# The FFN's first weight factors, moments and z tiles made within the attention's last heads

## The chip, the cores and the metric

One core of a Trainium2 chip runs the whole program. The time is the device time of one execution in microseconds; lower is better. In this text a microsecond is us.

## The reference, cut to what matters

A transformer block with both branches fed by the same layer norm, four batches of 512 tokens.

```python
# L0_attn_x (4, 512, 512); hidden 512, 16 heads of 32, inter 2048
x = L0_attn_x
xn = _layernorm(x)
x = x + attention(xn, Wq, bq, Wk, bk, Wv, bv, Wo, bo) + ffn(xn, gate_cp, up_cp, down_cp)

# attention
q, k, v = proj(Wq, bq), proj(Wk, bk), proj(Wv, bv)
scores = q @ k.T / sqrt(32) + slope[h] * arange(1 - s, 1)   # causal: masked above the diagonal
ctx = softmax(scores) @ v
attn = ctx @ Wo + bo

# ffn: each dense weight is a Catmull-Rom spline through 8134 control points
def spline_reconstruct(control_points, out_size, in_size):
    n = out_size * in_size
    idx, f = _catmull_rom_grid(control_points.shape[0], n)
    p0, p1, p2, p3 = control_points[idx[0]], ..., control_points[idx[3]]
    w = 0.5 * (2*p1 + (p2 - p0)*f + (2*p0 - 5*p1 + 4*p2 - p3)*f**2 + (3*p1 - p0 - 3*p2 + p3)*f**3)
    return w.reshape(out_size, in_size)
inter = silu(xn @ gate_w.T) * (xn @ up_w.T)      # gate_w, up_w (2048, 512)
ffn = inter @ down_w.T                           # down_w (512, 2048)
```

## The kernel before, in words

The program has two blocks, `attention` and `ffn`, each with one hand-written instruction stream per engine (TensorE PE, VectorE DVE, ScalarE ACT, GpSimd POOL, SyncE SP, which issues the DMAs). All engines meet at a barrier between the two. Inside a block only semaphores order the engines; every engine runs its own stream strictly in order.

Every fp32 product is made of two rounded parts, high and low, and three matmuls (high x high, high x low, low x high). So each operand costs a copy on ACT (high) and a subtraction on DVE or POOL (low).

**Attention.** It goes over batches b = 0..3 and heads s = 0..15. One `step(b, s)` does the scores of head s (L513), the exponentials on ACT (L901), transposes the probabilities of head s-2 (`turn_probs`, L527) and multiplies those of head s-3 with the values (`weigh_values`, L544 and L547). Projections of later heads and batches are laid into the steps by the tables `UNITS` and `TURNS`. For the last batch the tables run dry: from step 8 on only the last q and k columns, the turns of the context and the output projection are left. Three extra steps (16 to 18) drain the last heads; `project_out` and `add_residual` (L751) end the block. Three PSUM banks (`pj_bank`) go round for all projections; `PJ_LAST` lists the order in which the last batch uses them. `stack` on SP copies q and k of four heads to their stacked form by three DMAs each (L1048); the fourth stack of a batch serves heads 12 to 15. `load_early` then brings the FFN's mask, the first three `factor`/`taps` chunks and the moment basis `bm_early` into room that the q, k and v weights no longer need.

**FFN.** The weights are never dense in the gate and up products. Four moments per piece of the normalised input ("mom": 21 matmuls with `bm`, L1279 to L1281, their high and low parts, a store to DRAM) and windows of it are loaded as the tile `z` (L1535 windows, L1557 moments); small factors `wgu_hi`, `wgu_lo` multiply it (`gate_up`, "gu", L1303 and L1304, 4 matmuls). The factors come in chunks: seven DVE or POOL operations blend a chunk of `taps` with its `factor` (`taps_op`, L1232 four products and L1237 three sums), ACT rounds (`taps_high`, L1352), DVE or POOL takes the low part (`taps_low`, L1250), and SP copies the halves across partitions (`copy_across`, L1519 or L1524). Chunk 0 gives `coef`, from which the dense down weight is made tile by tile ("gen": `make_down`, 4 matmuls with `bd`, L1291 and L1292; ACT L1358, DVE `merge` L1418, ACT L1367, DVE L1422). Chunks 1 to 4 give the gate and up factors of four tiles each. `down` (12 matmuls, L1316 to L1318) adds a tile to the output.

There are 64 FFN steps k, 16 tiles g for each of four batches t; batch t = 0 is attention batch 3. `ffn_order()` writes PE's order: for t = 0 each step is gu(k), down(k-2), gen(k+2), and the moments of the next batch stand behind two of the steps. Two pairs of PSUM banks alternate; `room_for` makes PE wait until the pair's last user is read. Before, POOL blends chunks 1 and 4, DVE chunks 0, 2 and 3. SP's FFN stream is one list of waits and DMAs; a wait in it holds all that follows.

## Time and profile before

| | us |
|---|---|
| median of 3 runs | 844.9 (841.9 to 845.68) |
| profiled execution, whole time | 845.87 |
| its span, first to last instruction | 844.1 |
| PE busy in the span | 703.6 (83%) |
| DVE, ACT, POOL busy | 505.1, 439.5, 354.6 |

The span is what the engines' records cover; the whole time is 1.8 us longer. The profiled execution lies 1.0 us above the median of the three runs. In the page's row of 40 slices of 21.1 us each, PE's digit is 8 or 9 nearly everywhere, 4 and 1 in two slices in the middle, at the change from attention to FFN. Matmuls overlap in the records (one lasts 0.39 us, the next starts after 0.23 us), so a stretch's rate is read from its count.

### The profile page before, as it was taken

The page shows a single profiled execution, that of the slowest core. Times are in us where ns is not written, and L with a number is a line of the kernel's source. Part 1 is how long each engine was busy: PE and PEld are TensorE (multiplying, and loading weights), DVE is VectorE, ACT ScalarE, POOL GpSimd, SP SyncE. Part 2 cuts the span into 40 slices and gives each one's busy share as a digit, 9 for nine tenths or more (in the row PEclk, how much of TensorE's full clock was granted, in tenths as well). Part 3 has the DMA queues.
Part 4 walks back from the last instruction along what each step waited for, and adds up shares of the span by engine and source line. Part 5 has one row for each costly group of instructions (what it writes and reads, how often), then busy time and mean ns, then how long its engine had stood idle before and what let it go on. Part 6 is the DMA issues. An engine that isn't in the chain of part 4 may idle for free. (4 is left out here: it accounts for less than half of the span.)

```text
span 844.1 us, 14059 instructions
## 1 busy us (share of the span) xinstructions
PE 703.6 (83%) x4884; PEld 558.1 (66%) x4884; DVE 505.1 (60%) x1273; ACT 439.5 (52%) x961; POOL 354.6 (42%) x207
## 2 busy tenths in 40 slices
PE   5677879889789898798898684169895999999997
PEld 4566657667567676576776563147684888888886
DVE  5286687779968888877798767185341321221212
ACT  4267566677748776666778751135441233233221
POOL 2343363445535444634455435145223334434434
PEclk9879689999989999899899798569997999999999
DMA  7982564454585336644545917664617545434401
GB/s 252 207 205 37 101 92 153 58 88 75 114 202 76 50 69 134 92 153 58 89 73 124 319 74 246 230 212 136 184 23 228 174 148 175 140 92 138 133 1 50
DMA packets 53024, 109.79 MB, mean 130 GB/s; under 512 B 6361, under 2 KB 6617, under 8 KB 51417
## 3 DMA queue, kind: packets, MB, share of 16 engines
q1 hardware_dynamic: 52808, 108.82, 51.6%
q8 instruction: 39, 0.64, 0.4%
q14 instruction: 33, 0.26, 0.1%
q10 hardware_dynamic: 144, 0.07, 0.0%
HBM read 59.32 MB, written 25.17 MB: 100 GB/s over the span
## 5 line engine op out<-in xcount | busy, mean ns | idle before, releaser
L988 POOL TENSOR_TENSOR work<-work 128x1280 f16<-128x1280 f32 x64 | 168.4, 2630 | 228.3 <-DVE work L714 228.1
L901 ACT ACTIVATE work<-work,neg_max 128x128 f32<-128x128 f32 (+3 forms) x256 | 142.2, 564 | 105.5 <-DVE neg_max L706 104.7
L706 DVE CUSTOM_DVE_ANT_0 work<-bank,dist 128x128 f32<-128x128 f32 (+3 forms) x256 | 115.4, 487 | 82.5 <-PE bank L513 68.2
L1476 POOL TENSOR_TENSOR in_lo<-inner,in_hi 128x512 fp32r<-128x512 f32 x64 | 84.0, 1313 | 180.5 <-ACT in_hi L1379 180.5
L1430 DVE TENSOR_TENSOR inner<-bank,silu 128x512 f32<-128x512 f32 x64 | 44.1, 689 | 135.7 <-ACT silu L1373 122.4
L910 ACT COPY work<-bank 128x768 f16<-128x768 f16 (+1 forms) x128 | 110.3, 909 | 28.5 <-PE bank L527 27.2
L527 PE MATMUL bank<-ident,work 128*128 128x128 f16 x1280 | 109.9, 231 | 10.3 <-DVE work L721 8.5
L513 PE MATMUL bank<-k_stack,q_stack 96*128 96x256 f32 (+2 forms) x256 | 81.6, 397 | 41.5 <-issue 22.5
L1379 ACT CAST in_hi<-inner 128x512 fp32r<-128x512 f32 x64 | 39.8, 621 | 146.4 <-PE bank L1318 137.6
L527 PEld LDWEIGHTS bank<-ident,work 128*128 128x128 f16 x1280 | 78.6, 103 | 50.4 <-issue 33.2
L1316 PE MATMUL bank<-w_room,in_hi 128*128 128x512 f32 x256 | 100.9, 394 | 0.4 <-POOL in_lo L1476 0.4
L1317 PE MATMUL bank<-w_room,in_hi 128*128 128x512 f32 x256 | 100.4, 392 | 0.0
L1318 PE MATMUL bank<-w_room,in_lo 128*128 128x512 f32 x256 | 100.3, 392 | 0.0
L513 PEld LDWEIGHTS bank<-k_stack,q_stack 96*128 96x128 f32 x256 | 48.9, 212 | 59.4 <-issue 31.2
L544 PE MATMUL bank<-v_parts,work 128*128 128x96 bf16 x640 | 68.1, 215 | 5.1 <-issue 3.9
L1303 PE MATMUL bank<-z,wgu_hi 128*128 128x512 f32 x128 | 52.2, 408 | 19.1 <-DMA z<-moment_scratch 9.3
L472 PE MATMUL bank<-xt_room,w_room 128*128 128x512 f32 x128 | 61.9, 484 | 5.1 <-DVE v_room L682 3.2
L547 PE MATMUL bank<-v_parts,work 128*128 128x64 bf16 x640 | 65.4, 199 | 0.0
L544 PEld LDWEIGHTS bank<-v_parts,work 128*128 128x128 f16 x640 | 53.8, 103 | 9.3 <-issue 4.7
L1316 PEld LDWEIGHTS bank<-w_room,in_hi 128*128 128x128 f32 x256 | 48.7, 190 | 11.5 <-POOL in_lo L1476 1.3
L1317 PEld LDWEIGHTS bank<-w_room,in_hi 128*128 128x128 f32 x256 | 48.7, 190 | 10.3
L1318 PEld LDWEIGHTS bank<-w_room,in_lo 128*128 128x128 f32 x256 | 48.5, 189 | 10.3
(101 smaller groups left out, 1429.0 us busy)
## 6 DMA issues: line engine op xcount, KB each, us to landing
q_stack<-parts SPq DMA_DIRECT2D x48, 256.0 KB, 5.6
k_stack<-parts SPq DMA_DIRECT2D x48, 256.0 KB, 5.6
z<-xt_scratch SPq DMA_DIRECT2D x128, 88.0 KB
x_in<-x SPq DMA_DIRECT2D x32, 256.0 KB, 5.7
xt_scratch<-xt_room SPq DMA_DIRECT2D x8, 1024.0 KB, 6.8
xt_room<-xt_scratch SPq DMA_DIRECT2D x6, 1024.0 KB, 8.2
factor<-c_basis SPq DMA_DIRECT2D x5, 1024.0 KB, 9.7
taps<-windows SPq DMA_DIRECT2D x5, 1024.0 KB, 11.6
```

The costliest lines, as they stand in the source:

```text
L513: pe.matmul(score_bank[i % 2][:, 0:n], q_stack[:, c % 2, h, i * P:(i + 1) * P], k_stack[:, c % 2, h, 0:n], start=True, stop=True).then_inc ...
L527: mm = pe.transpose(pt_bank[i % 2][:, (part * n + k) * P:(part * n + k + 1) * P], probs16[:, s % 2, part, OFF[i] + k * P:OFF[i] + (k + 1) ...
L544: pe.matmul(bank[:, i * 96:(i + 1) * 96], probs_t[:, s % 2, at:at + P], v_parts[:, k, s, :, :], start=(k == 0), stop=False)
L547: mm = pe.matmul(bank[:, i * 96:i * 96 + 64], probs_t[:, s % 2, at:at + P], v_parts[:, k, s, 0:2, :], start=False, stop=(k == n - 1))
L706: dve.tensor_tensor_reduce(probs[:, s % 2, OFF[i]:OFF[i] + n], score_bank[i % 2][:, 0:n], dist[:, S - n:S], -slope(s), 3.4e38, ALU.add, AL ...
L901: e = act.activation(tile, tile, ACT.Exp, bias=neg_max[:, s % 2, i:i + 1], scale=-1.0, accum_out=row_sum[:, s % 4, i:i + 1])
L910: act.copy(probs_t[:, s % 2, 2 * OFF[i]:2 * OFF[i] + n], pt_bank[i % 2][:, 0:n]).then_inc(pt_free[i % 2], 1)
L988: pool.tensor_tensor(probs16[:, s % 2, 1, :], probs[:, s % 2, :], probs16[:, s % 2, 0, :], ALU.subtract).then_inc(lo_ready, 1)
L1316: pe.matmul(sum_bank[i][:, :], hi, wd_hi[:, g, :], start=(g == 0), stop=False)
L1317: pe.matmul(sum_bank[i][:, :], hi, wd_lo[:, g, :], start=False, stop=False)
L1318: mm = pe.matmul(sum_bank[i][:, :], lo, wd_hi[:, g, :], start=False, stop=(g == NG - 1))
L1476: pool.tensor_tensor(in_lo[:, k % 2, :], inner[:, k % 2, :], in_hi[:, k % 2, :].bitcast(F32), ALU.subtract).then_inc(il_ready, 1)
```

## The change

SBUF rooms of the FFN are placed by hand at offsets from the end of the common rooms, over attention tensors by when these are last read: `wgu_hi` over `q_stack`, `wgu_lo` over `k_stack`, `bd` and `z` over the probabilities and values, `coef` over `dist` and `bv_all`, and `in_lo` in two pieces.

- `load_basis` (the moment basis and `factor` 2) is issued ahead of the last `stack`; the mask goes behind chunks 0 and 1.
- PE makes the last batch's three moments at the ends of steps 12, 13 and 14 (9, 9 and 3 matmuls); ACT takes the high part in the same step, DVE the low part at the end of the next. SP stores them, and then loads the first `bd` quarter, the windows of z tiles 0 to 3 once all probabilities are transposed, their moments, and the second `bd` quarter, all within the attention block.
- DVE blends chunks 0 and 1 in steps 17 and 18 and between the last four residual sums; ACT rounds them and issues their copies on its own DMA queue, behind the loading of the Silu table.
- In the FFN, chunks 2, 3 and 4 all go through DVE by the table `TAPS`, spread over steps k = 0 to 10; POOL blends nothing. The next batch's moments move from behind steps 8 and 9 to behind 11 and 13.
- SP's list for t = 0 is rewritten: loads of z tiles, chunks and copies alternate; `bm`, the next batch's `xt_room`, the residual and the last `bd` quarter now stand together ahead of the last copy.

The diff, cut to its core ("..." where lines are left out; the helpers `taps_op`, `tiles_of`, `taps_low`, `load_windows` and `load_moments` moved out of `ffn` with their bodies as they were):

```diff
+        base = aligned(nc)
+        room = lambda name, shape, dt, at: nc.alloc_sbuf_tensor_at(name, shape, dt, offset=base + at * KB)
+        wgu_hi = room("wgu_hi", [P, 2, NG, P], F32R, 0)
+        wgu_lo = room("wgu_lo", [P, 2, NG, P], F32R, 16)
+        bd = room("bd", [P, 2, 4, 2, P], F32R, 32)
+        z = room("z", [P, NG, S], F32R, 42)
+        coef = room("coef", [P, 2, 512], F32R, 74)
+        in_lo = [room("in_lo0", [P, S], F32R, 78), room("in_lo1", [P, S], F32R, 40)]
...
+        def load_basis(sp):
+            sp.wait_ge(bases_st, 16)
+            sp.dma_start(bm_early[:].bitcast(F32).rearrange("p k e n -> p (k e n)"), moment_d).then_inc(bme_ld, 16)
+            sp.dma_start(factor[2][:], c_factor[2]).then_inc(chunk_ld[2], 16)
+
         def load_early(sp):
 
-            sp.dma_start(mask.bitcast(U32).rearrange("p g n -> p (g n)"), c_mask).then_inc(mask_ld, 16)
             for c in range(2):
                 sp.dma_start(factor[c][:], c_factor[c]).then_inc(chunk_ld[c], 16)
                 sp.dma_start(taps[c][:], cpts[c]).then_inc(chunk_ld[c], 16)
-            sp.wait_ge(bases_st, 16)
-            sp.dma_start(bm_early[:].bitcast(F32).rearrange("p k e n -> p (k e n)"), moment_d).then_inc(bme_ld, 16)
-            sp.dma_start(factor[2][:], c_factor[2]).then_inc(chunk_ld[2], 16)
+            sp.dma_start(mask.bitcast(U32).rearrange("p g n -> p (g n)"), c_mask).then_inc(mask_ld, 16)
...
+        def copy_across(eng, c):
+
+            eng.wait_ge(made_lo[c], 2)
+            for m in range(2):
+                own, other = slice(m * ZR, (m + 1) * ZR), slice((1 - m) * ZR, (2 - m) * ZR)
+                if c == 0:
+                    eng.dma_start(coef[other, m, :].bitcast(F32), in_lo[0][own, :].bitcast(F32)).then_inc(dup_ld[0], 16)
+                    continue
+                for each in (wgu_hi, wgu_lo):
+                    tiles = each[:, m, 4 * (c - 1):4 * c, :].rearrange("p g n -> p (g n)")
+                    eng.dma_start(tiles[other].bitcast(F32), tiles[own].bitcast(F32)).then_inc(dup_ld[c], 16)
...
+MOMENTS = {12: 0, 13: 1, 14: 2}
+PJ_LAST = [("q", 3), ("k", 3), ("c", 1), ("m", 0), ("m", 1), ("m", 2), ("c", 2), ("o", 0), ("o", 1), ("c", 3), ("o", 2), ("o", 3)]
...
+            def moment(m):
+                bank, used = pj_use(("m", m), B - 1)
+                pe.wait_ge(pj_free[bank], used)
+                if m == 0:
+                    pe.wait_ge(bme_ld, 16)
+                some = [(n, c) for n, (of, c) in enumerate(BM_PAIRS) if of == m]
+                for n, c in some:
+                    first, last = n == some[0][0], n == some[-1][0]
+                    pe.matmul(pj_bank[bank][:, :], bm_early[:, n, 0, :], xt_hi[:, c, :], start=first, stop=False)
+                    pe.matmul(pj_bank[bank][:, :], bm_early[:, n, 0, :], xt_lo[:, c, :], start=False, stop=False)
+                    mm = pe.matmul(pj_bank[bank][:, :], bm_early[:, n, 1, :], xt_hi[:, c, :], start=False, stop=last)
+                mm.then_inc(pj_full, 1)
...
+                if s in MOMENTS:
+                    moment(MOMENTS[s])
...
+                if s - 1 in MOMENTS:
+                    moment_low(MOMENTS[s - 1])
+                if s == H + 1:
+                    for n in range(4):
+                        taps_op(dve, 0, n)
+            for n in range(4, 7):
+                taps_op(dve, 0, n)
             ctx_low(B - 1, KC - 1)
-            for q in range(QT):
-                add_residual(B - 1, q)
+            taps_op(dve, 1, 0)
+            add_residual(B - 1, 0)
+            dve.wait_ge(ql_ready, 8 * B)
+            for m in range(2):
+                taps_low(dve, 0, m)
+            add_residual(B - 1, 1)
+            for n in range(1, 4):
+                taps_op(dve, 1, n)
+            add_residual(B - 1, 2)
+            for n in range(4, 7):
+                taps_op(dve, 1, n)
+            add_residual(B - 1, 3)
+            for m in range(2):
+                taps_low(dve, 1, m)
...
+            def moment_high(m):
+                bank, _ = pj_use(("m", m), B - 1)
+                act.wait_ge(pj_full, pj_total(("m", m), B - 1))
+                if m < 2:
+                    act.wait_ge(stacked[m][(KC - 1) % 2], 2 * STACK * B)
+                else:
+                    act.wait_ge(mom_sv[0], 32)
+                act.copy(parts[:, 2 * (m % 2), :], pj_bank[bank][:, :]).then_inc(mom_hi, 1)
...
+            act.wait_ge(t_done, 4 * H * B)
+            taps_high(act, 0)
             act.activation(warm[:], ident[0:1, 0:1], ACT.Silu)
+            copy_across(act, 0)
+            act.wait_ge(s_full, 4 * H * B)
+            taps_high(act, 1)
+            copy_across(act, 1)
...
+            load_basis(sp)
             stack(B - 1, 3)
...
+            for m in range(3):
+                bank, used = pj_use(("m", m), B - 1)
+                sp.wait_ge(pj_free[bank], used + 1)
+                per = 8 if m < 2 else 4
+                for e in range(2):
+                    sp.dma_start(mom_d[2 * (B - 1) + e, :, 8 * m:8 * m + per, :],
+                                 parts[0:NG * per, 2 * (m % 2) + e, :].bitcast(F32)).then_inc(mom_sv[m % 2], 16)
+            sp.wait_ge(lo_ready, H * B)
+            load_pieces(sp, 0)
+            sp.wait_ge(pt_full, QT * H * B)
+            sp.wait_ge(xt_st, 32 * B)
+            sp.wait_ge(pad_st, 16)
+            for g in range(4):
+                load_windows(sp, 0, g)
+            sp.wait_ge(mom_sv[0], 64)
+            sp.wait_ge(mom_sv[1], 32)
+            load_moments(sp, 0, 0)
+            load_pieces(sp, 1)
             for q in range(QT):
...
-    order = [("mom", 0, 0, 0), ("mom", 0, 1, 1), ("gen", 0, 0, 1), ("gen", 1, 0, 1)]
+    order = [("gen", 0, 0, 1), ("gen", 1, 0, 1)]
...
-        if t < B - 1 and g in ((8, 9) if t == 0 else (6, 8)):
-            half = 0 if g == (8 if t == 0 else 6) else 1
+        if t < B - 1 and g in ((11, 13) if t == 0 else (6, 8)):
+            half = 0 if g == (11 if t == 0 else 6) else 1
...
+TAPS = {0: [(2, i) for i in range(4)], 1: [(2, i) for i in range(4, 7)], 2: [(2, 7), (3, 0)], 3: [(3, 1), (3, 2)],
+        4: [(3, 3), (3, 4)], 5: [(3, 5), (3, 6)], 6: [(3, 7), (4, 0)], 7: [(4, 1), (4, 2)], 8: [(4, 3), (4, 4), (4, 5)],
+        9: [(4, 6)], 10: [(4, 7)]}
+HIGHS = {1: 2, 5: 3, 9: 4}
...
             sp.dma_start(taps[2][:], cpts[2]).then_inc(chunk_ld[2], 16)
-            sp.wait_ge(xt_st, 32 * B)
-            sp.wait_ge(pad_st, 16)
-            for q in range(QT):
-                sp.wait_ge(res_st[q], 16 * B)
-            load_pieces(0)
-            for g in range(4):
-                load_windows(0, g)
-            load_chunk(4)
-            load_pieces(1)
-            load_chunk(3)
-            copy_across(0)
-            for m in range(3):
-                store_moment(0, m)
-            load_moments(0, 0)
-            copy_across(1)
-            sp.dma_start(bm[:].bitcast(F32).rearrange("p k e n -> p (k e n)"), moment_d).then_inc(bm_ld, 16)
-            copy_across(2)
-            load_xt(1)
             for g in range(4, 8):
                 load_windows(0, g)
             load_moments(0, 1)
+            for q in range(QT):
+                sp.wait_ge(res_st[q], 16 * B)
+            load_chunk(3)
+            copy_across(sp, 2)
+            sp.dma_start(taps[4][:], cpts[4]).then_inc(chunk_ld[4], 16)
+            for g in range(8, 12):
+                load_windows(0, g)
+            load_moments(0, 2)
             load_pieces(2)
             sp.wait_ge(made[3], 4)
-            sp.nop(nofuse=True)
+            sp.dma_start(factor[4][:], c_factor[4]).then_inc(chunk_ld[4], 16)
+            copy_across(sp, 3)
+            for g in range(12, NG):
+                load_windows(0, g)
+            load_moments(0, 3)
+            sp.dma_start(bm[:].bitcast(F32).rearrange("p k e n -> p (k e n)"), moment_d).then_inc(bm_ld, 16)
+            load_xt(1)
+            sp.wait_ge(made[4], 4)
             load_mid(0)
-            copy_across(3)
-            sp.wait_ge(made_lo[4], 2)
-            sp.nop(nofuse=True)
-            for g in range(8, 16):
-                load_windows(0, g)
-                if g % 4 == 0:
-                    load_moments(0, g // 4)
-            copy_across(4)
             load_pieces(3)
+            copy_across(sp, 4)
```

DVE at the end of the attention, before: the low part of the last context column, then the four residual sums.

```order
L744 TENSOR_TENSOR ctx_t<-bank,ctx_t 128x512 [waits ch_ready]
L751 TENSOR_TENSOR x_in<-bank,x_in 128x512 [waits res_ld0,pj_full]
L751 TENSOR_TENSOR x_in<-bank,x_in 128x512 [waits res_ld1,pj_full]
L751 TENSOR_TENSOR x_in<-bank,x_in 128x512 [waits res_ld2,pj_full]
L751 TENSOR_TENSOR x_in<-bank,x_in 128x512 [waits res_ld3,pj_full]
```

DVE at the same place after the change (`taps_52` is chunk 0, `taps_53` chunk 1; four products of chunk 0 stand one head earlier):

```order
L335 TENSOR_TENSOR taps_52<-taps_52 128x512 [waits made0] x3
L846 TENSOR_TENSOR ctx_t<-bank,ctx_t 128x512 [waits ch_ready]
L330 TENSOR_TENSOR taps_53<-taps_53,factor_50 128x512 [waits chunk_ld1]
L853 TENSOR_TENSOR x_in<-bank,x_in 128x512 [waits res_ld0,pj_full]
L355 TENSOR_TENSOR in_lo_61<-taps_52,coef 64x512 [waits made_hi0,ql_ready]
L355 TENSOR_TENSOR in_lo_61<-taps_52,coef 64x512 [waits made_hi0]
L853 TENSOR_TENSOR x_in<-bank,x_in 128x512 [waits res_ld1,pj_full]
L330 TENSOR_TENSOR taps_53<-taps_53,factor_50 128x512 x3
L853 TENSOR_TENSOR x_in<-bank,x_in 128x512 [waits res_ld2,pj_full]
L335 TENSOR_TENSOR taps_53<-taps_53 128x512 [waits made1] x3
L853 TENSOR_TENSOR x_in<-bank,x_in 128x512 [waits res_ld3,pj_full]
L355 TENSOR_TENSOR wgu_lo<-taps_53,wgu_hi 64x512 [waits made_hi1] x2
```

Between and behind the residual sums now stand the blends of both chunks and their low parts; the last two rows before the barrier are chunk 1's low parts, each 64 rows high.

SP in the FFN's first batch, before: what stands around the last `bd` quarter, which PE's gen 12 to 15 need.

```order
L1535 DMA z<-xt_scratch 44x1x512 x8
L1557 DMA z<-moment_scratch 20x4x512 x2
L1535 DMA z<-xt_scratch 44x1x512 x6
L1524 DMA wgu_hi<-wgu_hi 64x512 [waits made_lo4]
L1524 DMA wgu_lo<-wgu_lo 64x512
L1524 DMA wgu_hi<-wgu_hi 64x512
L1524 DMA wgu_lo<-wgu_lo 64x512
L1509 DMA bd<-bases_scratch 128x1024 [waits gen_full]
```

SP after the change, around the same load:

```order
L367 DMA wgu_hi<-wgu_hi 64x512
L367 DMA wgu_lo<-wgu_lo 64x512
L317 DMA z<-xt_scratch 44x1x512 x8
L322 DMA z<-moment_scratch 20x4x512 x2
L1669 DMA bm<-bases_scratch 128x1792
L1634 DMA xt_room<-xt_scratch 128x4x512 x2
L1642 DMA resid<-mid_scratch 128x512 [waits made4]
L1642 DMA resid<-mid_scratch 128x512 x3
L309 DMA bd<-bases_scratch 128x1024 [waits gen_full]
L367 DMA wgu_hi<-wgu_hi 64x512 [waits made_lo4]
```

The last `bd` quarter stood behind z windows and a copy; it now stands behind z windows, the basis `bm`, two loads of `xt_room` and four of `resid`. The copy of chunk 4 stands behind it.

## Rows read from the trace of the kernel before

**Rows 1.** Windows view: us, busy time and count of each engine, PE clock, DMA.
```profile
517.70:539.80 22.10, 0.01 (x1) 0.01 (x1) 10.05 (x10) 1.82 (x3) 6.20 (x4) 0.57 0.89 319
539.80:564.10 24.30, 11.41 (x24) 6.66 (x24) 14.83 (x21) 7.60 (x13) 7.04 (x5) 0.57 0.50 144
564.10:637.80 73.70, 70.21 (x293) 56.11 (x293) 36.34 (x51) 35.26 (x61) 26.34 (x19) 0.97 0.48 141
637.80:647.10 9.30, 0.06 (x1) 0.01 (x1) 0.00 (x0) 0.62 (x1) 6.13 (x5) 0.64 0.84 251
647.10:652.10 5.00, 4.98 (x15) 3.97 (x16) 0.69 (x1) 0.60 (x1) 0.00 (x0) 0.64 0.61 170
700.00:750.00 50.00, 49.78 (x220) 40.91 (x219) 12.01 (x18) 15.41 (x28) 20.54 (x17) 1.00 0.45 134
```

**Rows 2.** Timeline, PE: start, duration, instruction, idle before and its releaser.
```profile
472.84 0.77 PE L513 MATMUL bank<-k_stack,q_stack 96*128 96x256 f32 x2 [4.20 <-issue]
539.79 0.80 PE L1291 MATMUL bank<-coef,bd 128*128 128x512 f32 x1 [22.11 <-DVE mom_st L1409]
564.14 0.80 PE L1303 MATMUL bank<-z,wgu_hi 128*128 128x512 f32 x1 [0.80 <-DVE inner L1430]
600.89 0.50 PE L1279 MATMUL bank<-xt_room,bm 128*128 128x512 f32 x1 [1.51 <-DVE w_new L1418]
647.12 0.77 PE L1303 MATMUL bank<-z,wgu_hi 128*128 128x512 f32 x1 [9.27 <-DMA z<-moment_scratch]
```

**Rows 3.** Timeline, ACT and DVE, the FFN's start.
```profile
538.42 0.59 ACT L1345 CAST mom_st<-bank 128x512 fp32r<-128x512 f32 x1 [12.61 <-DMA moment_scratch<-mom_st]
541.90 0.59 ACT L1358 COPY w_new<-bank 128x512 f32<-128x512 f32 x1 [2.89 <-PE bank L1292]
542.59 0.72 DVE L1418 COPY_PREDICATED w_new<-v_room,bank 128x512 f32<-128x512 uint8 x1 [2.85 <-ACT w_new L1358]
```

**Rows 4.** Timeline, PE and DVE, between attention heads 14 and 15.
```profile
485.26 0.96 PE L527 MATMUL bank<-ident,work 128*128 128x128 f16 x14 [0.68 <-DVE work L721]
486.03 0.48 PE L513 MATMUL bank<-k_stack,q_stack 96*128 96x256 f32 x2
486.80 0.29 DVE L706 CUSTOM_DVE_ANT_0 work<-bank,dist 128x128 f32<-128x128 f32 x1
```

**Rows 5.** Timeline, DVE, the attention's last operation.
```profile
511.10 0.69 DVE L751 TENSOR_TENSOR x_in<-bank,x_in 128x512 f32<-128x512 f32 x1 [2.10 <-PE bank L474]
```

**Rows 6.** View of the tile taps: durations min/median/max in ns, first and last start.
```profile
L1232 DVE TENSOR_TENSOR taps<-taps,factor x12: 676/687/1825, 512.6 to 564.0; 128x512 f32<-128x512 f32 x12
L1232 POOL TENSOR_TENSOR taps<-taps,factor x8: 1280/1714/1737, 512.6 to 568.1; 128x512 f32<-128x512 f32 x8
```

**Rows 7.** Timeline, SP: start and duration of DMA issues.
```profile
448.48 3.63 SPq L1053 DMA_DIRECT2D x_in<-x  x4
458.65 1.87 SPq L1048 DMA_DIRECT2D q_stack<-parts  x3
464.28 2.97 SPq L1048 DMA_DIRECT2D k_stack<-parts  x3
547.06 0.60 SPq L1524 DMA_DIRECT2D wgu_lo<-wgu_lo  x1
630.50 0.36 SPq L1626 DMA_DIRECT2D bo_all<-bo  x1
631.98 6.76 SPq L1535 DMA_DIRECT2D z<-xt_scratch  x8
638.84 0.81 SPq L1557 DMA_DIRECT2D z<-moment_scratch  x2
```

**Rows 8.** DMA view, issues at 467.4, 470.3, 604.5 us: KB, us to landing.
```profile
v_room<-c_mask SPq DMA_DIRECT2D x1, 1024.0 KB, 7.7
...
factor<-c_basis SPq DMA_DIRECT2D x1, 1024.0 KB, 20.3
...
bd<-bases_scratch SPq DMA_DIRECT2D x1, 512.0 KB, 3.9
```

292 lines of the change are left out of this document (133 added, 159 removed).

## The prediction

> **What bounds the kernel now.** I read four views. First the page's row of 40 slices, to see where PE is idle: two slices at the change from attention to FFN. Then the windows view over these places [rows 1]: from 517.7 to 539.8 us PE does one matmul, from 539.8 to 564.1 it does 24, from 564.1 to 637.8 it does 293, then it stands 9.3 us. At full rate, 220 matmuls in 50 us give 0.227 us each. The last batches run at that rate, so work moved inside them gains nothing and only the idle stretches can be won. Third the timeline, for what ends each idle. PE's 22.1 us before 539.79 are put down to DVE's `mom_st` [rows 2]; ACT's row shows the true end: the third moment's high part waited 12.61 us for the store of the first, since `mom_st` has two slots [rows 3], and SP issued that store behind its list of loads. Beside it POOL and DVE blend together from 512.6 on, and an operation of DVE lasts up to 1.8 us instead of 0.69 [rows 6]. Fourth SP's timeline and the DMA view: the boundary to the second FFN batch waits for z's moments, issued at 638.84 as the end of a chain that begins when gen 15 ends, at 630.5 [rows 2, 7].
>
> **The change, part by part.** The sum is made against the profiled execution: 845.87 us, span 844.1.
>
> Attention, loads. `bm_early` and `factor` 2, 1.9 MB, now go out behind the residual loads, at about 452 us, ahead of the last q and k stacks (458.65 and 464.28). For the k stack PE waited 4.2 us, until 472.84 [rows 2, 7]. Seven loads that landed 7.7 us after 467.4 (the first) and 20.3 us after 470.3 (the last) moved 5.9 MB in 15.5 us, 2.65 us a MB [rows 8]; so 1.9 MB take 5.0 us and could be through when q's stack is issued at 458.7. Bounds 0 and 5 us; I take 1.0, as most of it falls in a gap.
>
> Attention, moments. A head's last transposes end at 486.03 where the next scores start; DVE takes these at 486.80, some 0.5 us after they are there, because it is itself busy [rows 4]. Nine matmuls are 2.05 us, so DVE starts 1.55 us late, less 0.25 in step 12, where it has a context column to finish. The 0.69 us low part fits into the wait of the following head. The last moment has three matmuls (0.7 us) that fit under DVE, but the low parts of the second and third then stand bare: 0.65 us each. Sum 1.3 + 1.6 + 1.3 = 4.2. ACT's three copies of 0.6 us lie in the same waits. Bounds: 1.9 (only the DVE operations) and 8 (whole matmul time plus all copies and low parts). PE's tail moves 5.2 us.
>
> Attention, tail. The last residual sum stood at 511.10 to 511.8, behind an idle of 2.1 us, as DVE has little to do there [rows 5]; the FFN began at 512.6 [rows 6]. DVE's blend of chunk 0 (products 2.5, sums 2.0) fits before and behind the normalising of head 15. Then DVE has, between the residual sums, 0.6 + 1.4 + 1.9 + 2.0 us, which keep up with PE until the third residual sum; the fourth ends at 518.0 instead of 517.0. Behind it: ACT's two casts, 0.6 each and starting at the same time as that sum (1.3); DVE's low parts 1.4; then ACT issues four copies at 0.6, 2.4; barrier 0.4 [rows 3, 6, 7]. FFN start at about 522.8, so +10.2 against 512.6. Bounds 517 (nothing of it bare) and 528. SP has 6.8 us of windows, moments and `bd` in hand from about 502 and is through before the last residual store.
>
> FFN start. gen 0 is PE's first instruction, at 522.9 instead of 539.79: gain 16.9. From gen 0 to gu(2) before: 564.14 - 539.79 = 24.35. Now, in order, at the low clock (four matmuls 2.1 us, 539.79 to ACT's start at 541.90): gen 0 2.1, ACT 0.6, merge 0.72, gen 1 beside which ACT rounds (to 5.6), gu(0), directly behind and so 0.4 shorter, to 7.3; ACT's second copy and merge to 7.1; rounding, silu, product to 9.2; DVE four products 2.5 and merge to 12.4; ACT's rounding and silu to 13.6; product to 14.5, gu(2). Every unit is from [rows 3, 6]; what is gone are the waits for POOL's low parts of chunk 1 and for their copy. Gain 9.85. At gu(2) the lead is 26.7.
>
> First FFN batch. 293 matmuls took 73.7 us before; at 0.227 they are 66.5, the rest is the low clock, two waits of 1.51 before the moments [rows 2] and small ones. The moments move but stay two waits. DVE per step: 0.69 + 0.74 + 0.69 and at most three blends, 4.2 of 4.54 us, so it holds. The copy of chunk 2 lands about 1.0 late for gu(4). What POOL loses there nobody waited for.
>
> The last `bd` quarter. From gu(6), in us: product 2.3, low parts 1.4, four copies 2.4, windows 6.8, moments 0.8, `bm` at 13.7, `xt_room`, `resid`, then `bd` at 17.4. In front of it in the queue are 0.9 + 2 + 1 MB; with its own half 4.4 MB x 2.65 = 11.6, so it lands at 25.3 to 27.7. PE needs it for gen 12 at 4 x 4.54 + 0.9 + 2.7 = 21.8. Bounds: in an empty queue it lands 3.9 us after issue [rows 8], no wait; at the other end 10. I take 4.7.
>
> What does the clock do in that wait? After 9.3 us idle, PE did 15 matmuls in 5.0 us instead of 22 at a granted clock of 0.64, 1.6 us lost [rows 1]; after 1.51 us at 600.89 it lost nothing. 4.7 lies between, and I add the 1.6 (sum 6.3), because the idle stretch from 517.7 on has the low clock in most of it. The Trainium skill ("TensorE: Matmul & The Clock Gate", What's actually happening) says the clock falls back after the array has been idle for a while and is released by activity. By it a wait of 4.7 us costs the 1.6 too; a shorter wait, under the lower bound of the landing, costs none.
>
> Boundary. Before: gen 15's end, 0.05 to `bo_all`, `xt_room`, windows 6.76, moments, landing: 16.6 us, of which PE had 7.3 of work [rows 2, 7]. Now the second half of the moments stands behind gen 15: a wait of 1.5, 0.7 of matmuls, ACT 0.6, DVE 0.7, two stores 1.2 on SP before that chain starts. That is 4.7 us more for SP against 2.2 for PE in the same place (already counted): gap 9.3 becomes about 11.5, cost 2.2, bounds 0 and 5. Later batches are the same code.
>
> Sum: 26.7 - 1.0 - 6.3 - 2.2 = 17.2. 845.9 - 17.2 = 828.7 for the profiled execution, which stood 1.0 above the median: 827.7.
>
> **Rivals.**
> (a) The `bd` load passes the backlog and lands in time. For it: z windows of one queue come in among larger loads; against it: the seven loads of [rows 8] landed in their order. Gain 6.3 more: 821.
> (b) The stacks wait behind the 1.9 MB by the full 5 us and the blends' tail runs to 528: 4 + 5 lost, 837. For it: PE waits for the k stack already. Against it: the 6 us between their issue and q's stack.
> (c) DVE becomes the bound. It now blends chunk 4 too while POOL makes `in_lo`. If its 27 blends and low parts in steps 0 to 10 took 1.75 us as beside POOL before, not 0.69 [rows 6], a step with two blends needs 2.1 + 3.5 = 5.6 us against 4.54, one with three 7.4: over the eleven steps 9 steps lose 1.1 to 3, some 18 in all, and the ramp 4. The gain turns into a loss: 850. It decides from 1.5 us a blend on. Against it: POOL works 1.3 us in a step of 4.54, after DVE's turn. The Trainium skill ("GPSIMD Engine Reference", Specifications) says that GpSimd shares its SBUF interfaces with VectorE when the latter's operation has two SBUF inputs, as every blend has. By that rule, each collision is real, and the times of 1.7 agree; what it leaves open is how many there are.
> (d) The change doesn't do what it says: something loaded early (chunk 0, a moment's store that ACT waits for in step 14) comes late and attention stalls. Half of the lead at gu(2) goes: 840.
>
> **Chances.** Forecast 0.50 (own range 824 to 832), (a) 0.22, (b) 0.12, (c) 0.04, (d) 0.08, smaller mixtures 0.04. About 0.5%, 4 us, is what a measurement can tell. Faster by more than that is everything but (c), part of (d) and the rest: 0.92; within 0.03, slower 0.05. The range reaches from (a) with a light attention to (b): 817 to 838.
>
> **What would show it.** Right: gen 0 near 523, gu(2) near 537, a PE wait for DMA `bd` at gen 12 around 577, a gap of 11 to 12 us before the second batch, ending near 630. Wrong: gen 0 after 530; DVE blends of 1.7 us between k = 0 and 10; no wait at gen 12; a PE idle of several us in heads 12 to 15.

## The result and the profile after

| | before | after |
|---|---|---|
| median, us (14 runs each) | 844.98 (840.85 to 847.82) | 839.96 (837.12 to 842.63) |
| profiled execution, whole time | 845.87 | 842.63 |
| its span | 844.1 | 840.8 |

The ratio of after to before is 0.9941, 95% interval 0.9924 to 0.9957: 5.0 us faster, where 17.2 were forecast, and outside the range (817 to 838). The profiled execution of after stands 2.7 us above its median, so the account below is made against 842.63 and the forecast's 828.7, which is 13.9 us apart.

The windows view of the changed kernel, over the stretches that answer to [rows 1]: the attention's end, gen 0 to gu(2), gu(2) to the end of the first batch, the gap (PE's idle ahead of the second batch), and 5 us behind it. A row holds the stretch and its length, the busy time and count of PE, its weight loads, DVE, ACT and POOL, PE's mean granted clock (1.00 is 2.4 GHz, 0.50 is 1.2), the busy share of the DMA engines and their GB/s.

```profile
509.84:524.87 15.03, 7.40 (x30) 5.51 (x31) 10.22 (x16) 3.81 (x6) 0.00 (x0) 0.90 0.66 191
524.87:540.06 15.19, 9.45 (x24) 5.73 (x24) 8.88 (x13) 5.15 (x10) 1.59 (x1) 0.72 0.79 261
540.06:630.90 90.84, 75.13 (x293) 58.48 (x293) 47.22 (x66) 36.41 (x63) 21.02 (x14) 0.89 0.47 143
630.90:643.04 12.14, 0.00 (x1) 0.03 (x1) 0.00 (x0) 0.62 (x1) 6.13 (x5) 0.65 0.90 286
643.04:648.04 5.00, 5.00 (x12) 3.94 (x13) 0.69 (x1) 0.60 (x1) 0.00 (x0) 0.50 0.65 189
```

The first two rows carry the gain: 24 matmuls that took 24.3 us now take 15.19, and PE's idle of 22.1 us is 6.8, so that gu(2) comes 24.1 us sooner (540.06 for 564.14). The third gives most of it back: the same 293 matmuls take 90.84 us instead of 73.70. PE's timeline says where; these rows answer to [rows 2].

```profile
474.40 0.77 PE L600 MATMUL bank<-k_stack,q_stack 96*128 96x256 f32 x2 [4.41 <-issue]
524.87 0.76 PE L1414 MATMUL bank<-coef,bd 128*128 128x512 f32 x1 [6.80 <-PEq L474]
540.06 0.79 PE L1426 MATMUL bank<-z,wgu_hi 128*128 128x512 f32 x1 [0.64 <-DVE inner L1542]
596.79 0.76 PE L1414 MATMUL bank<-coef,bd 128*128 128x512 f32 x1 [10.05 <-DMA bd<-bases_scratch]
606.06 0.50 PE L1402 MATMUL bank<-xt_room,bm 128*128 128x512 f32 x1 [1.86 <-DVE w_new L1530]
643.04 0.77 PE L1426 MATMUL bank<-z,wgu_hi 128*128 128x512 f32 x1 [12.14 <-DMA z<-moment_scratch]
```

The first row is the restart behind the k stack, the second gen 0, the third gu(2), the fourth gen 12, the fifth the first moments of the second batch, the last that batch's gu(0). gen 0 (forecast 522.9) and gu(2) (forecast 537.4) are 2.0 and 2.7 us late. From gu(2) to the restart at 643.04 it takes 103.0 us, before it took 83.0 [rows 2], and the forecast was 92.5. So 10.5 of the 13.9 us are lost in the first FFN batch, and the wait of 10.05 for `bd` is the largest piece. SP's timeline shows how that load came so late.

```profile
568.96 0.54 SPq L367 DMA_DIRECT2D wgu_hi<-wgu_hi  x1
...
571.47 6.56 SPq L317 DMA_DIRECT2D z<-xt_scratch  x8
578.08 0.88 SPq L322 DMA_DIRECT2D z<-moment_scratch  x2
579.00 0.35 SPq L1669 DMA_DIRECT2D bm<-bases_scratch  x1
579.40 0.96 SPq L1634 DMA_DIRECT2D xt_room<-xt_scratch  x2
580.41 4.57 SPq L1642 DMA_DIRECT2D resid<-mid_scratch  x4
585.03 0.50 SPq L309 DMA_DIRECT2D bd<-bases_scratch  x1
```

gu(6) stood at 562.50. The copies were issued 6.5 us behind it (3.7 in the forecast's list). From `bm` to `bd` it is 6.0 us, most of it the four `resid` loads (3.7 in the forecast), and `bd` landed 11.8 us behind its issue.

### The profile page after: what moved, and what is told of

Read it like the earlier page. It is cut to its first block and busy times, and to the rows that moved or that the text cites. A ratio compares the mean times of both kernels' runs of the same rounds, so it can differ in the third digit from the quotient of the medians.

```text
span 840.8 us, 14002 instructions
## 1 busy us (share of the span) xinstructions
PE 707.4 (84%) x4884; PEld 561.4 (67%) x4884; DVE 507.8 (60%) x1289; ACT 439.6 (52%) x961; POOL 332.6 (40%) x191
## 5 line engine op out<-in xcount | busy, mean ns | idle before, releaser
L1579 POOL TENSOR_TENSOR in_lo<-inner,in_hi 128x512 fp32r<-128x512 f32 x64 | 85.8, 1342 | 230.1 <-ACT in_hi L1497 230.1
L1439 PEld LDWEIGHTS bank<-w_room,in_hi 128*128 128x128 f32 x256 | 49.2, 192 | 11.8 <-POOL in_lo L1579 1.3
```

The costliest lines, as they stand in the source:

```text
L1439: pe.matmul(sum_bank[i][:, :], hi, wd_hi[:, g, :], start=(g == 0), stop=False)
L1579: pool.tensor_tensor(in_lo[k % 2][:, :], inner[:, k % 2, :], in_hi[:, k % 2, :].bitcast(F32), ALU.subtract).then_inc(il_ready, 1)
```

## The experiments

Every ratio is to the kernel before, on the same chip, with its 95% interval; the changed kernel alone is 0.9941 (0.9924 to 0.9957). A thousandth is 0.84 us. A, B and C are the theories of the expectation printed above each result. Where the interval of an experiment overlaps that of the kernel it starts from, the times alone don't show its gain, and the reading rests on the profile.

**1. `bd` early.** In SP's list of the first batch:

```
 copy_across(sp, 3)
+load_pieces(3)
 ...
 load_mid(0)
-load_pieces(3)
```

> One move on the sync engine's list of the first FFN batch: the load of the last quarter of bd stands right behind the copy of chunk 3, ahead of the windows of z 12 to 15, bm, xt_room and resid, instead of behind them all. Theory A (the wait at gen 12 is the backlog of 3.9 MB in front of bd plus its late issue, and nothing else stands behind it): bd is issued near 570 instead of 585 and is there long before gen 12, PE's wait of 10.05 us goes, and with it the low granted clock of 596.8 to about 605, worth 3 to 4 us more. The windows and bm then land about 1.5 us later, still ahead of their use. Gain 12 to 14 us against the changed kernel: 826 to 828, ratio to the kernel before about 0.979. Theory B (something else is as late as bd: the second moments' xt_room, or z 12 to 15, behind the same backlog): PE waits there in its place, gain under 5 us, 835 or more. Theory C (the time is set by how much the queue moves between 570 and 597, since the moments of the second batch need bm and xt_room anyhow): the boundary gap of 12.1 us grows by what gen 12 gains, 838 to 841.

Measured 0.9825 (0.9797 to 0.9852), 830.0 us: 9.8 us better than the changed kernel. PE's wait for `bd` is gone; gu(2) to the next batch's start is 91.5 us instead of 103.0. From PE's timeline, the two longest waits behind gu(2):

```profile
596.09 0.50 PE L1402 MATMUL bank<-xt_room,bm 128*128 128x512 f32 x1 [1.86 <-DVE w_new L1530]
...
632.28 0.77 PE L1426 MATMUL bank<-z,wgu_hi 128*128 128x512 f32 x1 [11.37 <-DMA z<-moment_scratch]
```

What follows: `bd`'s place cost 10 to 11.5 us, clock included. That is A with less gain than it said: it laid the low clock from 596.8 to about 605 on this wait, but in the changed kernel's profile the clock is back at 1.00 from 601 to 606 and falls a second time at the moments, as it does here. B and C are out: nothing took the wait's place, and the gap did not grow.

**2 and 3. `bd` in two places between.** In the first it stands ahead of the four `resid` loads, in the second ahead of `xt_room` too.

```
 load_xt(1)                    +load_pieces(3)
 sp.wait_ge(made[4], 4)         load_xt(1)
+load_pieces(3)                 sp.wait_ge(made[4], 4)
 load_mid(0)                    load_mid(0)
-load_pieces(3)                -load_pieces(3)
```

> From the changed kernel, bd's last quarter goes one place forward: ahead of the four resid loads (1 MB), still behind bm and xt_room (3 MB). It is issued at about 580.4 instead of 585.0. Theory A (bd lands when what is queued in front of it has moved, at the 0.31 to 0.39 MB a us that the engines move from 580 to 595): 3.4 MB and the rest of z's windows take some 10 to 11 us from 580, so it lands at 590 to 592 instead of 596.8; PE's wait falls from 10.05 to 4 or 5 us, and still brings the low clock: gain 5 to 6, ratio about 0.987. Theory B (a wait of half the length brings none of the low clock): gain 8, 0.984. Theory C (the landing is set by the slow transfers beside it, not by its place): gain under 2, 0.993.

> bd's last quarter one place further forward: behind bm (0.9 MB) and ahead of xt_room and resid. Theory A (place in the queue): issued at 579.4, lands at 584 to 585, ahead of PE's need at 586.7: no wait, the same as when it stood behind the copy of chunk 3, ratio 0.982 to 0.983. Theory B (z 12 to 15 and xt_room then become what PE waits for): a wait of some us at gu 12 or at the second batch's moments, ratio 0.986 or more.

Measured 0.9892 (0.9860 to 0.9923) and 0.9811 (0.9776 to 0.9846). PE's timeline of the one and of the other:

```profile
592.38 0.77 PE L1414 MATMUL bank<-coef,bd 128*128 128x512 f32 x1 [5.85 <-DMA bd<-bases_scratch]
```
```profile
585.94 0.47 PE L1414 MATMUL bank<-coef,bd 128*128 128x512 f32 x1 [0.95 <-DMA bd<-bases_scratch]
```

The wait goes 10.05, 5.85, 0.95, 0 as the load moves forward from the changed kernel's place, and the issue 22.5, 18.0, 16.9, 9.0 us behind gu(6). From the first place to the second it is issued 4.6 us sooner and lands 12.0 instead of 11.8 us later, though 1 MB less stands in front: what counts there is the issue. Ahead of `xt_room` it lands 8.2 us behind its issue. What is measured is the place in the list (A). Between the first two, 4.2 us less wait gave 4.1 us by the ratios. The profiles show the clock's share: from gen 12 to the first moments it takes 9.27 us behind the wait of 10.05, 8.93 behind 5.85 and 7.56 behind 0.95, where the clock stays at 1.00. So the low clock costs 1.7 us after the longest wait and 1.4 after the middle one (B fell).

**4. The windows of the second batch early.**

```
 copy_across(sp, 4)
+for g in range(4):
+    load_windows(1, g)      # no longer behind the moments' stores
```

> One move: the windows of z 0 to 3 of the second FFN batch are loaded right behind the copy of chunk 4, ahead of the stores of the second batch's moments and of bo_all and xt_room, instead of behind them. Theory A (the gap of 12.14 us before the second batch is the chain stores, bo_all, xt_room, eight window loads at 0.85 us, moments, landing on the one issuing engine): the eight issues, 6.7 us, leave the chain, the moments are issued at about 628 instead of 634.6, and the gap falls to about 6, plus less time at the low clock: 833 to 834. Theory B (the landing of the z moments waits for the 2 MB of xt_room in front of it in the queue): 2 MB at 2.65 to 4 us a MB are 5 to 8 us from 626.9, so the moments land at 632 to 635 plus their own whatever their issue; the gap shrinks by some 3 to 6. Theory C (the gap has its cause in the moments themselves): no change, 840.

Measured 0.9906 (0.9872 to 0.9940), 3.0 us, the gap 7.99 instead of 12.14.

```profile
638.12 0.77 PE L1426 MATMUL bank<-z,wgu_hi 128*128 128x512 f32 x1 [7.99 <-issue]
```

That is B: the issues left the chain, and 2.2 MB in front of the moments took their place. The moments are issued at 627.20, and PE starts 10.9 us behind that.

**5. The moments ahead of those 2.2 MB as well.**

```
 store_moment(1, 2)
+load_moments(1, 0)
 bo_all <- bo ; load_xt(2)
 ...
-load_moments(1, 0)
```

> From the changed kernel, only the boundary: z's windows 0 to 3 of the second batch behind the copy of chunk 4, and its first moments loaded right behind their last store, ahead of bo_all and the 2 MB of xt_room for the third batch. Theory A (with the windows moved alone, ratio 0.9906, the gap fell only from 12.1 to 8.0 us, since the moments then waited for bo_all and xt_room in the queue: 2.2 MB, issued at 609.9 and moments landed 10.8 us behind their issue in the kernel with four moves): the moments are issued 1.6 us earlier and land in about 3 us, so that the gap falls to about 1 and the low clock behind it goes: 10 to 13 us below the changed kernel, 828 to 830, ratio about 0.981. Theory B (the gap is then set by the stores' own chain, since the last store is issued at about 625 and must land before the moments are loaded, 3 + 3 us): gap 2 to 4, 831 to 833, ratio 0.985. Theory C (z 4 to 7 or xt_room come late instead): PE waits later in the second batch, 835 or more.

Measured 0.9811 (0.9779 to 0.9844), 11.0 us.

```profile
631.10 0.47 PE L1426 MATMUL bank<-z,wgu_hi 128*128 128x512 f32 x1 [1.43 <-issue]
```

The gap is 1.43 us instead of 12.14, the whole of A; the moments are issued at 626.71, 4.4 us ahead of that start.

**6. The moments one head earlier in attention.**

```
-MOMENTS = {12: 0, 13: 1, 14: 2}
+MOMENTS = {11: 0, 12: 1, 13: 2}
```

> The three early moments stand one head earlier in attention: the first behind step 11, where PE waits 4.4 us for the k stack, the second in step 12, the third in step 13. Theory A (what the moments cost in attention is PE time, and the first cost double since it ran at the low clock that followed that wait): the first one fills the wait, step 12 carries 9 matmuls at nearer full clock, step 13 three. Before the move heads 12, 13 and 14 were 3.8, 1.6 and 0.5 us longer; now 0, 1.6 to 2.5 and 0.5, so the FFN starts 3 to 4 us earlier, near 521: 836 to 837. Theory B (it is the copies and low parts on ACT and DVE that lengthen the heads): they are all still there, gain below 1 us. Theory C (the low clock comes from the wait for the k stack however it is filled): step 12 stays slow, gain about 2.

Measured 0.9918 (0.9891 to 0.9944). PE's wait for the k stack is 1.86 us, as the nine matmuls now stand ahead of it (1.98 and 3.52 in experiments 10 and 11, which have this move too), and the three heads from 12 to 15 take 15.6 us instead of 18.5. But from head 15's first operation on DVE to the last `ctx_t` it takes 18.9 us instead of 17.0, so most of that is given back. By the ratio 1.9 us are gained, but the two intervals overlap: likely, not shown.

**7. A third of the moments' matmuls.**

```
-some = [... for n, (of, c) in enumerate(BM_PAIRS) if of == m]
+some = [... if of == m][:1]
```

> The first and second early moment in attention are made of 3 matmuls each instead of 9, so this kernel leaves out two thirds of their sums; everything else (copies, low parts, stores, loads) stays. Theory A (a head of attention is longer by the matmul time of its moment, at whatever clock it then runs): in the changed kernel the first moment's nine took 2.86 us from 479.44 to 482.30, most of it at the low clock, the second's 2.05. Without six of each, 1.4 to 2.2 and 1.4 us go: gain 3 to 3.5, some 836.5. Theory B (DVE's and ACT's copies of the moments lengthen the heads): gain under 1 us, 839.5.

This kernel leaves out six of the nine matmuls of the first moment and of the second. Measured 0.9924 (0.9897 to 0.9950), again a difference inside the intervals; the profile tells more than the times. DVE's first operation in heads 12, 13 and 14, before:

```profile
473.53 0.29 DVE L706 CUSTOM_DVE_ANT_0 work<-bank,dist 128x128 f32<-128x128 f32 x1 [5.80 <-PE bank L513]
478.30 0.28 DVE L706 CUSTOM_DVE_ANT_0 work<-bank,dist 128x128 f32<-128x128 f32 x1
482.53 0.29 DVE L706 CUSTOM_DVE_ANT_0 work<-bank,dist 128x128 f32<-128x128 f32 x1
```

after, with head 15's:

```profile
475.08 0.29 DVE L808 CUSTOM_DVE_ANT_0 work<-bank,dist 128x128 f32<-128x128 f32 x1 [6.13 <-PE bank L600]
482.72 0.29 DVE L808 CUSTOM_DVE_ANT_0 work<-bank,dist 128x128 f32<-128x128 f32 x1 [2.79 <-issue]
488.78 0.29 DVE L808 CUSTOM_DVE_ANT_0 work<-bank,dist 128x128 f32<-128x128 f32 x1 [1.23 <-issue]
493.55 0.28 DVE L808 CUSTOM_DVE_ANT_0 work<-bank,dist 128x128 f32<-128x128 f32 x1
```

and with three matmuls a moment:

```profile
471.47 0.29 DVE L808 CUSTOM_DVE_ANT_0 work<-bank,dist 128x128 f32<-128x128 f32 x1 [6.29 <-PE bank L600]
476.34 0.29 DVE L808 CUSTOM_DVE_ANT_0 work<-bank,dist 128x128 f32<-128x128 f32 x1
481.10 0.27 DVE L808 CUSTOM_DVE_ANT_0 work<-bank,dist 128x128 f32<-128x128 f32 x1
```

Head 12 takes 4.77 us before, 7.64 after and 4.87 here; head 13 4.23, 6.06 and 4.76. In head 13 the clock is full in both, and six matmuls cost 1.3 us. In head 12 the 2.8 are not the matmuls alone: behind PE's restart the low clock lasts some 6.5 us in the changed kernel's profile and some 3.6 here (windows of 1 us). The kernel of experiment 2 has all nine matmuls, and there it lasts 3.7:

```profile
476.20 0.29 DVE L808 CUSTOM_DVE_ANT_0 work<-bank,dist 128x128 f32<-128x128 f32 x1 [6.32 <-PE bank L600]
482.48 0.29 DVE L808 CUSTOM_DVE_ANT_0 work<-bank,dist 128x128 f32<-128x128 f32 x1 [1.42 <-issue]
```

That head 12 takes 6.28 us, 1.4 more than with three. So the matmul time is what lengthens the heads (A), 1.3 to 1.4 us for six, and up to 1.4 more is the clock; the ten profiles that have all nine there show head 12 between 6.28 and 7.72 us.

**8. Basis loads behind the k stack.**

```
-load_basis(sp)
 stack(B - 1, 3)
+load_basis(sp)
```

> The loads of bm_early and factor 2 (1.9 MB) are issued behind the last k stack instead of in front of the last q and k stacks, still ahead of the other early loads. Theory A (in front, they cost the k stack more than the profile of the changed kernel shows: PE's wait for it was 4.41 us there, but 5.50, 6.27 and 8.25 in three kernels with the same code up to there, as the basis still moves when q's stack is issued): the wait returns to about 4.2 and the mean gain is 1.5 to 2.5 us, 837.5 to 838.5. bm_early lands at about 473 to 476, in time for the first moment at 479. Theory B (the wait for the k stack is lengthened by whatever is queued behind it, chunk 0's loads in the one case and the basis in the other): no change, 840. Theory C: bm_early comes late for the first moment and head 13 waits, 841 or more.

Measured 0.9966 (0.9947 to 0.9985), and PE's wait 4.46 us. No gain, by the middle value 2 us worse: A's gain is not there. The short wait that A named is, but it shows nothing: PE's wait for the k stack lay between 4.41 and 8.25 us (mean 5.7) in ten profiles whose code is the changed kernel's up to there, three of them under 4.5. What makes it vary was not settled.

**9. Chunk 1's copies in the FFN.**

```
 taps_high(act, 1)
-copy_across(act, 1)
 ...                          # first in SP's FFN list:
+copy_across(sp, 1)
```

> The four copies of chunk 1's factors to the other half of the partitions are issued by the sync engine as the first of the FFN, instead of by ACT in front of the barrier. Theory A (ACT's six DMA issues of 0.5 to 0.6 us stand bare between the last low part at 521.4 and the barrier): the FFN starts 2.2 us earlier, gen 0 at about 522.7, while the copies are issued from then on and land before gu(0) needs them, some 8 us behind gen 0: 837.5 to 838. Theory B (gu(0) then waits for the copies, 4 x 0.8 us of issue and 2 to 3 of landing, and chunk 2's taps come 3 us later to DVE): the gain is given back by gu(2), 840.

Measured 0.9905 (0.9876 to 0.9933), 3.0 us. The intervals overlap, but the profile shows the same 3.0:

```profile
518.71 0.76 PE L1413 MATMUL bank<-coef,bd 128*128 128x512 f32 x1 [3.81 <-PEq L474]
```

From the attention's last `ctx_t` (507.40) to gen 0 PE needs 11.3 us instead of 14.3, and gu(2) is 15.2 us behind gen 0 as in the changed kernel: A, nothing is given back.

**10. Four of these together** (1, 4, 6, 9).

> Four moves together, each tried alone before: bd's last quarter behind the copy of chunk 3 (ratio 0.9825 to the kernel before), z's first windows of the second batch ahead of its moments' stores (0.9906), the early moments one head earlier (0.9918), and chunk 1's copies issued by the sync engine in the FFN (0.9905). The changed kernel alone stands at 0.9941. If they are independent their gains add: 9.8 + 3.0 + 2.0 + 3.0 = 17.8, so 822 (0.973). If the earlier bd and the earlier windows meet in the same queue, or the first batch's start waits for chunk 1, a part is lost: 824 to 827.

Measured 0.9738 (0.9709 to 0.9767), 821.4 us, where the four gains one by one add up to 0.973: they add.

**11. All five** (with 5).

> All moves together: the four of the kernel at 0.9738 and the first moments of the second batch ahead of bo_all and xt_room. Theory A (the gap of 7.92 us there was the queue in front of the moments): it falls to 1 or 2, 7 to 9 us less with the clock: 812 to 814, ratio 0.963 to 0.965. Theory B (the wait only moves to z 4 to 7, which now have 2.2 MB in front of them, or to the moments of the third batch): 817 to 820.

Measured 0.9607 (0.9577 to 0.9636), 812.1 us, a little below A. The gap is 1.36 us.

**12 and 13. Gen ahead of down, then the moments ahead of both**, in the two steps that carry the second batch's moments.

```
 gu(k), down(k-2), gen(k+2), mom        # as it is
 gu(k), gen(k+2), down(k-2), mom        # 12, with bd early
 gu(k), mom, down(k-2), gen(k+2)        # 13, on all five
```

> bd's last quarter early as in the run before, and in the two steps with the second batch's moments the matmuls of gen stand ahead of those of down, so that down's 12 matmuls (2.7 us) lie between gen and the moments, which wait for gen's merge. Theory A (the waits of 1.86 and 1.50 us there are bare, and the first of them drops the granted clock, 0.60 in the 4 us behind it with 11 matmuls instead of 18): both waits go, 3.4 us, and 1.6 with the clock: 5 us below bd early alone, 825. Theory B (down then waits for DVE or ACT, which get the gen's work earlier and the product later): gain under 2 us, 828 or more. Theory C (the second batch's start hangs on the store chain on the sync engine and not on PE): 3.4 us go, but the gap before the second batch grows by 1.5 or more: 828.

> On the kernel with five moves (ratio 0.9607): in the two steps with the second batch's moments, these stand directly behind gu, ahead of down and gen, so that they wait for nothing (the pair of banks was merged a step before) and down's 2.7 us lie between them and gen, which needs the banks next. Theory A (the waits of 1.86 and 1.51 us go, and since no wait is left the clock does not fall behind the first: in the kernel with bd early it was 0.60 for 4 us with 11 matmuls instead of 18): 3.4 + 1.6 = 5 us, 807, ratio 0.955. Theory B (gen now waits for DVE's low parts of two moments, 0.6 + 0.7 + 0.7 behind PE's 4.1, less what down covers): the waits move, as they did with gen ahead of down: gain under 1.5, ratio 0.959 or more. Theory C (bm or xt_room is not there yet): a wait for DMA.

In both, A fell. The first is 0.9860 (0.9832 to 0.9888), no better than `bd` early alone, and its waits ahead of the moments are 2.43 and 2.08 us instead of 1.86 and 1.50. The second is 0.9660 (0.9636 to 0.9685), 4.5 us worse than the five. Its timeline has both of the rivals named, C and B:

```profile
586.13 0.77 PE L1401 MATMUL bank<-xt_room,bm 128*128 128x512 f32 x1 [2.85 <-DMA xt_room<-xt_scratch]
...
598.63 0.50 PE L1413 MATMUL bank<-coef,bd 128*128 128x512 f32 x1 [2.57 <-DVE mom_st L1520]
...
613.16 0.50 PE L1413 MATMUL bank<-coef,bd 128*128 128x512 f32 x1 [1.97 <-DVE mom_st L1520]
```

**14. Small blends.** On the changed kernel.

```
+w = slice(0, 8 if c > 2 else 512)
-taps[c][:, n, :] = taps[c][:, n, :] * factor[c][:, n, :]
+taps[c][:, n, w] = taps[c][:, n, w] * factor[c][:, n, w]   # sums alike
```

This kernel leaves out 504 of the 512 columns of every product and sum of chunks 3 and 4.

> From the changed kernel: the products and sums of chunks 3 and 4 are done on 8 of their 512 columns, so this kernel leaves out nearly all of that work on the vector engine; the casts, low parts, copies, waits and loads stay. Theory A (my rival of a bound vector engine, in a small size: between gu(3) and gu(8) a step takes 4.53 to 5.63 us, 25.6 us for the five of them, against 4.54 for one in which PE waits for nothing): the steps fall to 4.54 except where ACT's casts or the low parts stand, and the kernel gains 2 to 3 us, ratio about 0.991. The copy of chunk 3 is still issued at the same step, and PE's wait for bd stays near 10. Theory B (the longer steps come from ACT's two casts, which stand ahead of gen's copy, and from the clock): under 0.8 us, ratio 0.993 to 0.995.

Measured 0.9940 (0.9915 to 0.9965), the changed kernel's own. From gu(3) to gu(8) it is 24.9 us instead of 25.6. A fell, for these two chunks; chunk 2's blends were left whole.

**15. Casts behind gen's copy.** On all five.

```
 inner_high(n)
-if n in HIGHS: taps_high(act, HIGHS[n])
 ...
 down_start(n)
+if n - 2 in HIGHS: taps_high(act, HIGHS[n - 2])
```

> On the kernel with five moves (ratio 0.9607): ACT's two casts of chunks 2, 3 and 4 stand behind its copy of gen, in the 0.87 us in which it waits for the merge, instead of ahead of that copy. Theory A (ahead of it they delay gen's merge and with it the next product: the steps that carry casts take 5.2 to 6.3 us instead of 4.54): 0.6 to 0.9 us less in two or three steps, 2 us in all, ratio about 0.9585. Theory B (the vector engine's blends stand in the same steps and bound them): no change, 0.9607. Theory C (the copies of the chunks go out later and PE waits for them): slower by 1.

Measured 0.9566 (0.9542 to 0.9590), 808.6 us, the lowest; its interval touches that of the kernel with five moves (0.9577 to 0.9636). ACT's timeline of the changed kernel around gen 7 and, under it, of this one around the same chunk's casts:

```profile
562.93 1.26 ACT L345 CAST wgu_hi<-taps 64x512 fp32r<-64x512 f32 x2 [0.46 <-DVE taps L335]
564.22 0.59 ACT L1474 COPY w_new<-bank 128x512 f32<-128x512 f32 x1
565.67 0.62 ACT L1485 CAST w_room<-w_new 128x512 fp32r<-128x512 f32 x1 [0.87 <-DVE w_new L1530]
```
```profile
554.57 0.59 ACT L1473 COPY w_new<-bank 128x512 f32<-128x512 f32 x1 [0.23 <-PE bank L1414]
555.05 1.26 ACT L345 CAST wgu_hi<-taps 64x512 fp32r<-64x512 f32 x2
556.34 0.62 ACT L1484 CAST w_room<-w_new 128x512 fp32r<-128x512 f32 x1
```

The 0.87 us in which ACT waited for the merge now holds most of the casts: from the copy to its rounding it is 1.77 us instead of 1.45, for casts of 1.26. The windows from gu(2) to gu(12), first of the kernel with five moves, then of this one:

```profile
534.70:595.80 61.10, 55.45 (x219) 43.19 (x219) 40.51 (x56) 28.94 (x50) 17.00 (x11) 0.93 0.68 214
```
```profile
533.37:590.51 57.14, 54.35 (x219) 43.35 (x219) 40.21 (x56) 28.75 (x50) 17.21 (x11) 0.93 0.72 225
```

The same instructions take 4.0 us less, and the ratios differ by 3.5. The 4.0 lie in the steps that begin with gu(2), (3), (6), (7) and (10), 0.6 to 1.2 each. The largest is in part the profile's: gu(3) to gu(4) took 6.27 us with five moves, but 5.64 in most profiles with the casts in the old place.

**16. Both 13 and 15.**

> Both on the kernel with five moves: the casts behind gen's copy and the moments ahead of down. If each does what its first theory says, 5 + 2 = 7 us below 812: 805, ratio 0.953. If only the moments do: 0.955; if neither: 0.960.

Measured 0.9638 (0.9613 to 0.9663), between 13 and 15, as 13 alone loses.

## Why the prediction was wrong

By its own steps:

- **k stack, 1.0.** In this profile 0.3: 474.40 against 472.84, of which 1.2 stood already at 448 us (448.37 against 447.18), in code that had not changed. That 1.2 is the run's, and is in the 13.9. Over the ten profiles with this code, from that matmul to the restart it is 27.1 us on average, 1.5 more than in the one profile before, so this profile is a light one and the term was not too large.
- **Moments in attention, 4.2.** The three heads are 2.9, 1.8 and 0.5 us longer, 5.2 in all; the forecast had 1.3 for the first, 1.6 for the second and 1.3 for the bare low parts. The first is 2.9 because the low clock that the wait for the k stack left lasted some 6.5 us, before 3.8, which this term did not have; where it lasted 3.7 (experiment 7), the first is 1.5 longer.
- **Tail, gen 0 at 522.9.** Measured 524.87; less the 1.2, 0.8 late. The four copies on ACT cost 3.0 us (experiment 9) for the 2.4 that were forecast, which is most of it.
- **Ramp, 14.5.** Measured 15.19.
- **First batch, "DVE per step ... so it holds", and 1.0 for chunk 2.** DVE does hold (experiment 14), but ACT was left out. Its two casts stand ahead of gen's copy, and the step waits for that copy. From gu(2) to gu(8) it took 33.3 us, before 30.6: 2.7 for the 1.0. With the casts behind gen's copy (experiment 15) the same stretch takes 30.6 again.
- **The last `bd` quarter, 6.3. This is the step that failed, the largest single piece of the miss.** The mechanism was right in place and kind, a wait for DMA `bd` at gen 12. Its size is 10.05 instead of 4.7. Of the 5.4 that are missing, the late issue makes 5.1 (22.5 us behind gu(6) for 17.4: 2.8 before the copies, 2.3 in the `resid` issues) and the queue 2.7 (11.8 us from issue to landing, where 4.7 of wait meant 9.1); PE itself came 2.4 later (24.2 for 21.8). With the casts behind gen's copy the copies go out 5.3 us behind gu(6) instead of 6.5, so 1.2 of the late issue is ACT's order too. Taking the load forward gave back 9.8 by the ratios, 11.5 in the profiles. The 1.6 for the low clock behind the wait held: 1.7 (experiments 2 and 3), with 8 matmuls from 596.79 to 600 at 0.50. The Trainium skill ("TensorE: Matmul & The Clock Gate", What's actually happening) says that activity releases the throttle of an idle array; the trace agrees, as the clock is back at 1.00 from 601 to 606, where PE works again.
- **The moments behind `bd`.** "Stay two waits" cost more than that: the step of the first took 13.26 us, before 10.42. Its wait is 1.86 instead of 1.51, and behind it the clock falls a second time, so that the moments' matmuls take 5.83 us instead of 4.22: 1.6 that the forecast put at nothing. It does not hang on `bd`: with `bd` early the moments take 5.83 too, in experiment 3 they take 4.22 (see the last section). The rest of the 2.8 is the tail of the low clock behind `bd`, counted there.
- **Boundary, 2.2, gap 11.5.** Measured 12.14, so 2.9. The step was right. The gap that it took as given could be had almost whole, 11 us, as experiment 5 shows.

Together, to gu(2) 2.7; in the batch 5.4 for `bd` and 0.1 for its clock, 1.7 for the casts, 2.0 at the moments (0.4 of wait, 1.6 of clock), 0.7 at the boundary and 0.6 of small ones; behind it 0.8, where PE does 12 matmuls in the first 5 us instead of 15. That is the 13.9, within rounding. The 1.2 that the run brought and the clock's 1.6 at the moments differ from profile to profile; the medians are 12.3 us apart.

Of the rivals, (a) needed the `bd` load to pass what stood in front of it; it landed 11.8 us behind its issue, and in experiments 1 to 3 what helped was a place further forward. (b) did not happen in this profile (gen 0 at 524.87, k stack 0.3), and 1.5 on average is far from its 5. (c) is refuted by experiment 14 for chunks 3 and 4: two of their products in the batch last 1.67 us and one sum 1.78, and no measurable time hangs on them. (d) gave the right number, 840, for another reason: nothing that was loaded early came late. My range left out that two sizes, the issue and the landing, could both be at their far ends; the upper bound of the wait alone, 10, would have given 834 for the profiled execution, and with ACT and the moments 838.

## What to carry to other kernels

When work is moved off the critical path's head, its loads move in the queue of the one issuing engine, and what stood behind them becomes late. List each load by its due time and by the megabytes in front of it: here the order of a few loads was worth some 21 (experiments 1 and 5) of the 32 us between the changed kernel and the fastest one. Count the in-order engine that is least busy as well: two casts of 1.26 us together, on an ACT under half load, cost a step 0.5 to 0.9 us, since they stood ahead of the copy that the others waited for.
